# A double step's first score group is issued ahead of its first maxima pair, in an attention and feed-forward kernel

## What is computed

```
n = layernorm(x)
q, k, v = n Wq + bq, n Wk + bk, n Wv + bv
a = softmax(q k^T / 8) v        (per head, all 2048 keys)
x = x + layernorm(a Wo + bo)
x = x + layernorm(gelu((layernorm(x) U1) V1 + b1) U2 V2 + b2)
```

## Time and profile before

| | |
|---|---|
| median of 3 runs | 2533.64 us (2533.57 to 2534.62) |
| the profiled execution | 2539.57 us, span from first to last instruction 2537.8 us |
| TensorE matmul busy | 2433.8 us, 96% of the span |
| ScalarE busy | 2163.1 us, 85% |
| VectorE busy | 2070.6 us, 82% |
| GpSimd busy | 2008.5 us, 79% |

### The profile page before, as it was taken

How to read it: one execution, slowest core, us unless ns; L and a number is a source line. 1 busy time by engine, 2 the same in 40 slices (tenths; PEclk the granted TensorE clock), 3 DMA queues, 4 the chain that set the end, 5 groups by cost and what they waited for, 6 DMA issues and landing times.

```text
span 2537.8 us, 44015 instructions
## 1 busy us (share of the span) xinstructions
PE 2433.8 (96%) x15728; PEld 1197.3 (47%) x15728; DVE 2070.6 (82%) x3171; ACT 2163.1 (85%) x2454; POOL 2008.5 (79%) x1095
## 2 busy tenths in 40 slices
PE   4999999999999999999999999999999999998885
PEld 2454454545445454544545454454445454454332
DVE  6788888888888888888888888888888888888877
ACT  2788889888988889888888988888888888887884
POOL 1588888888888888888888888888888888887673
PEclk7899999999999999999999999999999999999997
DMA  1010001000000000100010000000001001000011
GB/s 40 18 31 18 22 26 32 14 26 26 25 21 26 26 14 26 31 26 14 26 32 21 20 26 26 19 26 26 26 14 31 26 18 29 26 26 22 26 34 29
DMA packets 60771, 63.11 MB, mean 25 GB/s; under 512 B 25900, under 2 KB 44204, under 8 KB 60556
## 3 DMA queue, kind: packets, MB, share of 16 engines
q1 hardware_dynamic: 60556, 60.30, 7.9%
HBM read 57.40 MB, written 2.62 MB: 24 GB/s over the span
## 4 chain that ended last, share of the span: by engine, by line
PE 85%; DVE 13%; issue 1%; ACT 1%; DMA 0%; POOL 0%; POOLq 0%; ACTq 0%; DVEq 0%
PE o_ps L361 37%; PE spare_ps L314 15%; PE score_ps L342 8%; PE score_ps L345 7%; PE score_ps L348 7%; DVE max_part L672 5%; PE spare_ps L282 2%; PE spare_ps L291 2%; PE spare_ps L300 2%; PE spare_ps L391 2%; DVE q_lo L694 2%; DVE k_lo L688 2%; PE spare_ps L373 1%; DVE ln_stats L629 1%; DVE z_sb L640 1%
## 5 line engine op out<-in xcount | busy, mean ns | idle before, releaser
L870 POOL TENSOR_TENSOR total<-total,probs 128x832 f32<-128x832 f32 x896 | 1767.1, 1972 | 364.2 <-ACT probs L541 290.9
L672 DVE TENSOR_REDUCE max_part<-spare_ps 128x1 f32<-128x512 f32 x2020 | 1309.5, 686 | 321.8 <-PE spare_ps L314 307.2
L541 ACT ACTIVATE probs<-score_ps 128x1024 f32<-128x1024 f32 x1024 | 994.9, 1022 | 263.0 <-PE score_ps L348 252.0
L531 ACT ACTIVATE score_ps<-m_all 128x1024 f32<-128x1024 f32 x1024 | 1011.6, 1032 | 7.6 <-PE score_ps L328 6.2
L361 PE MATMUL o_ps<-probs,v_sb 128*64 128x512 f32 x4096 | 998.3, 609 | 0.0
L314 PE MATMUL spare_ps<-k_hi,q_hi 64*128 64x512 f32 x2020 | 477.2, 467 | 29.0 <-DVE max_part L672 12.2
L361 PEld LDWEIGHTS o_ps<-probs,v_sb 128*64 128x64 f32 x4096 | 250.0, 137 | 451.7 <-issue 323.6
L342 PE MATMUL score_ps<-q_hi,k_hi 64*128 64x512 f32 x2048 | 417.8, 403 | 6.0 <-ACT score_ps L531 5.9
L345 PE MATMUL score_ps<-q_lo,k_hi 64*128 64x512 f32 x2048 | 406.5, 392 | 0.0
L348 PE MATMUL score_ps<-q_hi,k_lo 64*128 64x512 f32 x2048 | 406.2, 391 | 0.0
L703 DVE TENSOR_REDUCE part_sum<-probs 128x192 f32<-128x768 f32 x256 | 393.4, 1537 | 5.0 <-ACT probs L541 5.0
(11 more groups left out here) (87 smaller groups left out, 1085.4 us busy)
## 6 DMA issues: line engine op xcount, KB each, us to landing
m_all<-m_scratch SPq DMA_DIRECT2D x64, 512.0 KB, 3.7
denom<-denom_scratch SPq DMA_DIRECT2D x126, 128.0 KB, 2.9
xg<-in_L_attn_x SPq DMA_DIRECT2D x14, 256.0 KB, 3.0
block_out<-z_sb SPq DMA_DIRECT2D x8, 256.0 KB, 2.3
m_scratch<-max_rows SPq DMA_DIRECT2D x64, 4.0 KB
denom_col<-denom SPq DMA_DIRECT2D x63, 4.0 KB
denom_scratch<-denom_col SPq DMA_DIRECT2D x63, 4.0 KB, 1.4
w_qkv<-in_L_attn_Wk SPq DMA_DIRECT2D x8, 64.0 KB, 2.9
```

Source lines behind the costliest of these rows:

```text
L531: nc.scalar.activation(score_ps[st % 2][:], m_all[:, G % 2], ACT.Copy).then_inc(s["seed_done"], 1)
L541: nc.scalar.activation(probs[:, st % RING], score_ps[st % 2][:], ACT.Exp, scale=SCALE).then_inc(s["exp_done"], 1)
L672: nc.vector.reduce_max(max_part[:, G % 2, h, qt, kc:kc + 1], bank[max_bank(n, h)], AX.X).then_inc(s["max_done"], 1)
L870: nc.gpsimd.tensor_tensor(others(total[:, G % 2]), so_far, others(probs[:, st % RING]), ALU.add).then_inc(s["sum_done"], 1)
```

## The change

`scores(2n)` is issued before `max_pair(2n + 22)` and no longer after it. The second score group stays where it was, so that each of the two pairs of maxima now has one score group in front of it. No other engine's order changes, and the banks are dealt out as before.

```diff
                 me.ffn(n, 0)
+                me.scores(2 * n)
                 if 2 * n + LEAD < STEPS:
                     me.max_pair(2 * n + LEAD)
-                me.scores(2 * n)
                 me.scores(2 * n + 1)
                 if 2 * n + LEAD < STEPS:
                     me.max_pair(2 * n + LEAD + 1)
```

## The result

The changed kernel takes 2755.89 us (median of 4 runs, 2755.01 to 2757.47) against 2534.13 us before: 1.0873 times the time, 95% interval 1.0854 to 1.0892. That is 222 us more where 184 were forecast, and 1 us beyond the upper end of the range. The direction and the mechanism came out as written, and so did the cost of a double step with Q or K. The cost of a plain double step was forecast too small.

What follows compares the result with a forecast made beforehand. TensorE was taken to bound the kernel. 122 x 0.69 + 379 x 0.34 = 213 us, less 23 (seed waits) and 6 (prefetch already lost behind Q), gave +184 us: 2718 us, range 2665 to 2755.

Steps and rivals of the forecast that it cites:

- TensorE bounds the kernel, so a gap is paid in full: Steady part: TensorE has records 99% of the time and 85% of the chain, so any new gap costs its full length.
- The distance between the pairs is what changes: Between a double step's two maxima pairs: one score group (0.7 us) instead of two (1.4 us), with banks still being reduced.
- A double step with Q or K costs 0.69 us: In 122 double steps, the second pair waits for q_lo or k_lo; values move from a + 2.38 to a + 3.07.
- A plain double step costs 0.34 us: In 379 double steps, the second pair waits for a reduction: 0.24 us of waiting and 0.10 of lost prefetch.
- Low bound, no prefetch lost: At the values behind a waiting pair: weights still loaded ahead, 50 us less in all (501 x 0.10).
- The sum with 379 ns from the start of a pair to its reduction: Skill page's matmul figure replacing the measured 0.44 us: second pairs start 0.06 us earlier, estimate 2688 us.
- The seed waits go: TensorE's 93 waits for seeds vanish as the period grows beyond ScalarE's work, saving 0.25 us each, 23 us.
- VectorE keeps up: At the first reduction of a double step: VectorE's 4.09 us of work fits the new plain period of 4.27.
- The chain's share of VectorE, "well over 30%": In the chain that ended last: VectorE rises from 13%, every double step passing through a reduction.
- A clock that swings: Rival: TensorE's pauses lower its clock, each tenth of the steady part at 1.2 GHz adding about 220 us; chance 0.03.
- Only Q and K pay: Rival: reductions finish within one score group, so plain double steps cost nothing; +61 us, 2595 us; chance 0.05.

Runs made afterwards that it cites:

- e5_max_wait_first: The changed kernel with a maxima pair waiting only for the later reduction, or for the reduction ahead of another bank user: 2724.26 us, ratio 1.0740.
- e11_wait_first_before: The kernel before with the order of waits alone (a maxima pair waits for the reduction first, or only for it), no projection moved: 2529.46 us, ratio 0.9977.

## Why the prediction was right, and where it was not

- **TensorE bounds the kernel, so a gap is paid in full: right.** The parts of the change add up, and shortening the reduction takes the plain double steps' cost away.
- **The distance between the pairs is what changes: right.** 0.80, 0.43 and 0.69 stand in the timeline as worked out.
- **A double step with Q or K costs 0.69 us: right.** 1.84 us from pair to pair, and 0.67 in the kernel that changes these alone.
- **A plain double step costs 0.34 us: too low, and this is the step that failed.** The prediction took the 0.05 us between VectorE's end and the waiting pair from the only row at hand, q_lo's, and put it on the reduction. Behind a reduction it was 0.15, since there the wait that ends last is the separate one of two; 1.27 us lie from pair to pair where 1.17 were forecast. Without that case (run e5_max_wait_first) they are 1.18. 379 x 0.09 = 34 us of the 38 that were missing. No row of before showed a pair held up in that way, and the bounds should have reached above the value of the nearest row, not only below. There was one sign: in the earlier trace rows the values come 0.42 behind a pair, which the prediction put down to Q. That pair had its own two waits: it starts 0.15 behind the end of its reduction (1020.27 + 0.69 = 1020.96 in the earlier trace rows, to 1021.11). It is on time behind its score group, but its weight load starts only at 1021.07, 0.11 behind the reduction. With the reduction waited for first (run e11_wait_first_before; it ends at 1017.49 there) the weight load starts 0.05 behind it, the pair again 0.15, and the values come 0.33 behind the pair:

```profile
1017.54 0.19 PEld L322 LDWEIGHTS spare_ps<-k_hi,q_hi 64*128 64x128 f32 x2 [0.16 <-DVE max_part L680]
1017.64 0.39 PE L322 MATMUL spare_ps<-k_hi,q_hi 64*128 64x512 f32 x2
1017.97 1.08 PE L369 MATMUL o_ps<-probs,v_sb 128*64 128x512 f32 x4
```

- **Low bound, no prefetch lost: wrong in the timeline.** The values came 0.43 behind every pair that had waited.
- **The sum with 379 ns from the start of a pair to its reduction: not borne out.** The first reduction came 0.43 to 0.44 us behind its pair in every timeline here. The figure of the Trainium skill (TensorE: Matmul & The Clock Gate, Single matmul latency) is for one bf16 matmul to its result, so this does not contradict it.
- **The seed waits go: right.** The second group follows the pair at 0.23. The forecast that the list would show them near nothing was wrong, as told above: the row is of the weight loads. In the trace of before, late seeds had lengthened the distance of the two pairs by 0.25 us on average at d = 2 and by 0.14 at d = 7, some 24 us in all where the sum had 23.
- **VectorE keeps up: right.** It idles 0.25 us ahead of the first reduction in the step shown, behind a partial sum.
- **The chain's share of VectorE, "well over 30%": wrong.** It is 20%. Only one reduction of a double step is on the path: 501 x 0.69 = 346 us is 13% of the span, which is line 672's share.
- **The rivals.** A clock that swings did not come: the granted clock was 1.00 from 150 to 2600 us, with a pause of TensorE of 0.3 to 0.9 us in nearly every double step. The Trainium skill (TensorE: Matmul & The Clock Gate, A second HAM failure mode: psum-queue depth-cycling) tells of a kernel whose clock swung with small idle gaps between groups that cycle through PSUM banks; this trace does not agree with that for its own pauses. "Only Q and K pay" is what the short reduction makes true: a score group covers 0.92 us from pair to pair, and what a reduction needs beyond that is paid.

## What to carry to other kernels

Where buffers rotate among uses of two kinds, an order is good or bad by what lies between one use of a bank and its next, not by which result is wanted first; count it bank by bank. And work moved out of the way of one wait can have been the cover of another: the projections in front of the scores gave ScalarE the time for its seeds. When an instruction must wait for two semaphores, see in the trace which of the two it carries (here the one that is waited for first in the code), make that the one that ends last, or drop the one that is implied.

## What was not expected of the hardware

A wait of TensorE that became an instruction of its own (51 ns) delayed the matmul by 0.15 us behind the reduction's end when it was the last to be met, 0.05 when the weight load carried it, and nothing measurable when it was already satisfied. Dropping the implied wait, or swapping the two lines so that the reduction is waited for first, was worth 0.09 us in each plain double step of the changed kernel, 31.6 us in all. In the kernel before it only brings the values behind some pairs from 0.42 to 0.33 us, and is worth 6.
